# Eight-head cross-attention: where SP issues the weights of the next head among the spills and fetches

## The reference, cut to what matters

```python
Q = (img_embed @ Wq).reshape(B, -1, H, D).transpose(0, 2, 1, 3)
K = (sent_embed @ Wk).reshape(B, -1, H, D).transpose(0, 2, 1, 3)
V = (sent_embed @ Wv).reshape(B, -1, H, D).transpose(0, 2, 1, 3)
score = jnp.einsum('bhqd,bhkd->bhqk', Q, K) / math.sqrt(D)
score = jnp.where(mask, score, -jnp.inf)
attn = jax.nn.softmax(score, axis=-1)
ctx = jnp.einsum('bhqk,bhkd->bqhd', attn, V).reshape(B, -1, H * D)
out = ctx @ Wo + img_embed
# ... and a layer norm of out over the features
```

## Time and profile before

| | us |
|---|---|
| median of 3 runs | 522.12 |
| lowest, highest | 521.54, 522.39 |
| the profiled execution | 522.01 |
| its span | 520.2 |
| PE busy | 477.9 (92%) |
| DVE busy | 337.8 (65%) |
| ACT busy | 289.6 (56%) |
| POOL busy | 241.8 (46%) |

### The profile page before, as it was taken

One profiled execution on the slowest core, in us unless ns is written; L12 is line 12 of the kernel. 1 busy time (PEld: TensorE's weight loads), 2 busy tenths in 40 slices (PEclk: granted clock), 3 DMA queues, 4 the chain that ended last, 5 costly groups with the idle time before them and its releaser, 6 DMA issues.

```text
span 520.2 us, 7521 instructions
## 1 busy us (share of the span) xinstructions
PE 477.9 (92%) x2424; PEld 396.7 (76%) x2424; DVE 337.8 (65%) x681; ACT 289.6 (56%) x465; POOL 241.8 (46%) x136
## 2 busy tenths in 40 slices
PE   1989999987979999999999999999999999998992
PEld 0867787775868887888788878888888788777892
DVE  5999774655555657565756575667656675775357
ACT  4676475556554646565556565655656564635222
POOL 4646565438535353535353535363635453533004
PEclk9999999999989999999999999999999999999997
DMA  8313022678566566666566655665665665551002
GB/s 267 127 43 122 1 61 82 203 209 216 189 193 191 160 188 187 188 184 185 185 210 177 202 190 161 202 201 166 200 185 176 197 205 174 190 161 42 0 2 81
DMA packets 53975, 81.98 MB, mean 158 GB/s; under 512 B 5792, under 2 KB 43072, under 8 KB 53824
## 3 DMA queue, kind: packets, MB, share of 16 engines
q1 hardware_dynamic: 53632, 81.62, 51.2%
q10 hardware_dynamic: 320, 0.08, 0.1%
HBM read 49.16 MB, written 32.51 MB: 157 GB/s over the span
## 4 chain that ended last, share of the span: by engine, by line
PE 43%; issue 24%; POOL 15%; DVE 10%; ACT 4%; DMA 3%; SPq 1%; POOLq 0%; DVEq 0%; ACTq 0%
PE ps_scores L603 14%; POOL probs_t_lo L498 10%; POOL w_lo L430 3%; PE ps_o L625 3%; PE ps_o L629 3%; PE ps_o L627 3%; PE ps_o L628 3%; PE ps_o L626 3%; DMA ring<-in_weights_a 2%; PE ps_turn L619 1%; PE ps_task L551 1%; PE ps_task L553 1%; PE ps_task L552 1%; ACT probs L961 1%; DVE resid L1370 1%
## 5 line engine op out<-in xcount | busy, mean ns | idle before, releaser
L498 POOL TENSOR_TENSOR probs_t_lo<-probs_t_lo,probs_t_hi 128x1024 fp32r<-128x1024 f32 x60 | 143.8, 2397 | 197.5 <-ACT probs_t_hi L971 197.5
L971 ACT ACTIVATE probs_t_hi<-probs_t_lo 128x1024 fp32r<-128x1024 f32 x60 | 63.3, 1055 | 31.0 <-DMA probs_t_lo<-scratch 30.8
L625 PE MATMUL ps_o<-probs_t_hi,val_hi 128*128 128x512 f32 (+1 forms) x144 | 58.0, 403 | 8.0 <-POOL probs_t_lo L498 4.4
L1261 DVE RECIPROCAL row_inv<-row_sum 128x1 f32<-128x1 f32 x72 | 11.3, 159 | 75.4 <-PE ps_scores L603 67.2
L626 PE MATMUL ps_o<-probs_t_lo,val_hi 128*128 128x512 f32 (+1 forms) x144 | 56.8, 394 | 0.0
L629 PE MATMUL ps_o<-probs_t_lo,val_rem 128*128 128x512 f32 (+1 forms) x144 | 56.7, 394 | 0.0
L627 PE MATMUL ps_o<-probs_t_hi,val_lo 128*128 128x512 f32 (+1 forms) x144 | 56.7, 394 | 0.0
L628 PE MATMUL ps_o<-probs_t_hi,val_rem 128*128 128x512 f32 (+1 forms) x144 | 56.7, 394 | 0.0
L1298 DVE STREAM_TRANSPOSE probs<-probs 128x1024 f32<-128x1024 f32 x30 | 37.3, 1245 | 25.4 <-ACT probs L961 25.4
L603 PE MATMUL ps_scores<-key_hi,q_hi 128*128 128x512 f32 x144 | 46.6, 405 | 3.0 <-DVE neg_scores L1274 1.7
L1298 DVE STREAM_TRANSPOSE neg_scores<-neg_scores 128x1024 f32<-128x1024 f32 x30 | 37.2, 1241 | 13.9 <-ACT neg_scores L961 13.9
(11 more groups left out here) (247 smaller groups left out, 1096.7 us busy)
## 6 DMA issues: line engine op xcount, KB each, us to landing
probs_t_lo<-scratch SPq DMA_DIRECT2D x240, 128.0 KB, 2.9
scratch<-neg_scores SPq DMA_DIRECT2D x30, 512.0 KB, 3.8
scratch<-probs SPq DMA_DIRECT2D x30, 512.0 KB, 3.6
ring<-in_weights_a SPq DMA_DIRECT2D x9, 512.0 KB, 5.2
ring<-in_weights_b SPq DMA_DIRECT2D x9, 512.0 KB, 5.4
ring<-in_keys_t SPq DMA_DIRECT2D x4, 512.0 KB, 3.4
ctx_raw<-in_context SPq DMA_DIRECT2D x2, 768.0 KB, 9.5
ring<-in_context SPq DMA_DIRECT2D x16, 96.0 KB, 2.6
```

What stands on the lines that cost most here:

```text
L498: nc.gpsimd.tensor_tensor(pt_lo[b][:, t, :, :], pt_lo[b][:, t, :, :].bitcast(f32), pt_hi[b][:, t, :, :].bitcast(f32), ALU.subtract).then_i ...
L625: pe.matmul(o0, val_hi[b][:, kt, :], hi, start=first, stop=False)
L971: act.activation(pt_hi[b][:, t, :, :], pt_lo[b][:, t, :, :].bitcast(f32), ACT.Copy)\
```

## The change

In heads 1 to 6 the loads move to other places in SP's order. Before, A for the head after the next was issued behind `fetch(h, 4)` and B for the next head behind `fetch(h, 7)`. Now B for the running head is issued behind `fetch(h, 0)`, and A behind `fetch(h, 1)`. B for head 1, issued behind `fetch(0, 7)` before, goes behind `fetch(1, 0)`; B for the last head is issued behind `fetch(6, 5)`. In head 0 the places of `load_b(0)` and `load_a(1)` stay. The number of transfers, their bytes, the waits inside `load_a` and `load_b`, and all other engines' programs are unchanged.

```diff
                     fetch(h, j)
                     if h == 0 and j == 0:
                         load_b(0)
-                    if (j == 4 if h else j == 5) and h < HEADS - 2:
+                    if h and j == 0 and h < HEADS - 1:
+                        load_b(h)
+                    if (j == 1 if h else j == 5) and h < HEADS - 2:
                         load_a(h + 1)
-                    if j == 7:
+                    if h == HEADS - 2 and j == 5:
                         load_b(h + 1)
```

## The result

The changed kernel is slower: 538.84 us median of 6 runs (534.8 to 540.62) against 521.83 for the kernel before on the same chip (6 runs, 519.42 to 523.82), ratio 1.0327, 95% interval 1.0293 to 1.036. The forecast was 530.2 with a range of 523.5 to 535. The direction and the place were right, the size was not: +8.2 us were forecast and +17.0 came by the medians. The profiled execution took 540.41 us, 18.4 more than that of before.

A forecast was written before the change was run, and what follows sets the result against it. TensorE, busy 92%, was taken as the bound, so changes show as idle PE or lower clock. 522.01 - 7.0 (block 2) + 12.6 (waits at block 6) + 2.6 (clock) = 530.2 us, range 523.5 to 535.

The forecast's parts named there:

- the chain ahead of fetch 3: SP, heads 1 to 5: 22.3 us from gate to fetch 3; block 6 ready at gate + 30.45, wanted at 28.05.
- the clock behind the new gaps: PE after new waits at block 6: lower clock in head 1 and one of four others, 2 x 1.3 = 2.6 us.
- the plain pair of 5.5 us: SP's queue: fetch to fetch with a spill but no weights between takes 5.48 us, against 8.4 with weights.
- Part 1: Block 2, heads 1 to 6: block 7's weights leave, 8.9 us lost now, 1.9 kept in head 1, gain 7.0 us.
- the 1.9 forecast: Block 2 of head 1: PE still waits for the fetch issued at 140.40, 1.9 us lost with 0.2 for the gap.
- Part 2: Block 6, heads 1 to 5: both weights behind fetches 0 and 1 make waits, 3.0 + 4 x 2.4 = 12.6 us.
- The gate of 0.35 us: In an undisturbed head the fetch of block 0 goes out 0.35 us before scores of block 2.
- The last head: Block 2 of the last head: chain of 52.3 us against 52.7 for PE, so no wait.
- the gap of 1.51 us was followed by matmuls at the higher level: PE before 124.31 us: its matmul took 0.50 us, not the 0.77 behind the long gap of 3.05 us.
- The free place: Rival, chance 0.10: pairs with weights under 7.2 us, chain meets PE, only the 7.0 us gain is left, 515.0 us.
- The clock falls at every gap: Rival, chance 0.15: lower clock behind all five new gaps, 6.5 us in place of 2.6, total 534.1 us.

The follow-up runs named there:

- the second profile of the changed kernel: Changed kernel, unchanged, run again beside the kernel before on one chip: 533.57 us, ratio 1.032.
- the filler run: Changed kernel plus 8 extra unused matmuls on PE just before the value product of block 6 in heads 1 to 6: 530.35 us, ratio 1.026.
- half the bytes: Changed kernel with only columns 0 to 511 of 1024 of the weights of heads 1 to 6 loaded, at the same places: 515.08 us, ratio 0.9966.

## Why the prediction was right in kind and wrong in size

The direction and the mechanism, a wait at block 6 by the chain ahead of fetch 3, came true. Two terms of the sum failed: the clock behind the new gaps (2.6 us forecast, 7.8 measured), and the plain pair of 5.5 us, which took 7.2 to 7.5 in heads 1, 2 and 6.

**Part 1 (7.0 us forecast).** Block 2 of heads 2 to 6 lost 4.3 and now nothing; head 1 went from 4.55 to 0.7, its gap is 0.47 us. Together 8.2 gained. But this is a value of one profile: before, run again, loses 3.0 in all these places. The step behind it, a landing of 6.08 us in place of 4.5 with weights behind, is not a rule (the run with A behind fetch 3, and before, run again). And head 1's 0.7 in place of the 1.9 forecast is luck that was paid for in head 0: the clock fell there, PE came 1.6 us later to head 1 (its scores start at 133.79 and not at 132.16), and its wait shrank. In the second profile of the changed kernel, with no fall in head 0, block 2 of head 1 loses 1.7 us, near the forecast.

**Part 2, the mechanism.** Gate, pairs, landing, rounding, wait at block 6 of heads 1 to 5: all there. The gate of 0.35 us was measured at 0.35 to 0.36 in heads 2 to 6. Heads 3 to 5 had 22.0, 22.7 and 22.3 us to fetch 3 against 22.3, and lost 2.2, 3.0 and 2.5 us before the clock, against 2.4. Every experiment that took one set, or bytes, out of the chain ahead of fetch 3 took the waits at block 6 of heads 2 to 5 away; only in head 2 of two later runs did 0.2 and 1.7 us come back, behind a slow pair.

**Part 2, the size in heads 1 and 2 (a term of the sum).** The third pair, without weights, was forecast at 5.5 and took 7.47 in head 1 and 7.35 in head 2. So PE lost 5.2 in head 1 (3.7 at block 6, and 1.5 at blocks 4 and 5, nearly all of it by the minimum of block 5, which waits for spill 3) and 3.9 in head 2, against 3.0 and 2.4. The DMA view of the changed kernel from 165 to 172 us has spill 3 of head 1 in it (DMA share in tenths, GB/s, each in 40 slices, then the queues):

```profile
DMA  9999899689999989854000000000010000000001
GB/s 322 310 287 263 234 205 217 152 205 334 222 345 386 456 351 398 328 211 170 6 12 12 6 29 23 23 23 23 23 47 0 0 0 0 0 0 0 0 0 23
...
q8 instruction: 1, 0.02, 0.8%
...
scratch<-probs SPq DMA_DIRECT2D x1, 512.0 KB, 5.6
```

All but a trickle of 6 to 47 GB/s is over 3.3 us into the stretch, at 168.3; the trickle goes on for 2 us more, and the spill counts as landed only then, 5.6 us after issue, where the same spill in head 3 took 3.5. One transfer of instructions (q8) lies in that stretch. It lies in the 7.35 us pair of head 2 as well, and in the pair of fetches 6 and 7 of head 6 (7.25 us), and in no pair of 5.4 us of this trace. In the filler run, whose program for PE is longer, it falls in the pair before, and the third pair of head 2 takes 5.41. In other runs such a transfer also lay in pairs of 5.4, but there it came later. All 13 traces from head 1 on, for spills that SP issued right behind a fetch, with no weights between (us):

| from the issue of the spill to the start of q8 | from issue to landing | cases |
|---|---|---|
| 1.6 to 2.5 | 4.9 to 5.7 | 14 |
| 2.6 to 3.1 | 3.5 to 5.0 | 14 |
| 3.1 to 3.6 | 3.5 to 3.7 | 9 |
| none in the pair | up to 3.9 | the rest |

I take the late landing for one DMA engine that was held up by the instructions it moved. The order in time speaks for it, but no run moved or removed these transfers alone, so it is a likely cause and not a shown one.

**The last head (0 forecast, 1.9 measured).** The prediction had 52.3 us for the chain against 52.7 of PE. The pair of fetches 6 and 7 was in that sum with 5.5 us, took 7.25 as just said, and the pair with B ahead of it 9.00 and not 8.4; together that is over four times the half microsecond of room. With B one block earlier (518.71 us) the pair takes 5.51 us and the wait is gone, but so it is in the run with A behind fetch 3, where B stays. So the slow pair makes the wait, and the order isn't shown to make the slow pair.

**The clock (2.6 forecast, 7.8 measured).** This is the largest miss, 5.2 us. The step that failed is "the gap of 1.51 us was followed by matmuls at the higher level", from which I took four gaps of 2.2 to 2.4 us to be mostly safe. The changed kernel has that very gap in head 0, in a part that wasn't changed; timeline, then window:

```profile
124.45 0.79 PE L627 MATMUL ps_o<-probs_t_hi,val_hi 128*128 128x512 f32 x1 [1.50 <-POOL probs_t_lo L500]
...
124.00:128.00 4.00, 3.55 (x9) 2.83 (x10) 1.81 (x2) 2.71 (x6) 1.32 (x2) 0.57 0.58 183
```

The first matmul takes 0.79 us where it took 0.50 in the earlier trace rows, and the stretch has a clock of 0.57. The same gap left the clock alone in one execution and brought it down in another: over the 13 profiles, all with this gap of 1.5 us in head 0, the clock fell behind it in seven, and head 1 starts at 133.7 to 134.1 us in those that lost this time and at 132.2 to 132.6 in the six others. So 1.5 of the 18.4 us between the two profiles are chance and not the change, and 1.2 of them come back at block 2 of head 1 (part 1). In the changed kernel 2.00 us brought the clock down and 2.78 did not. One example of each kind is no bound; in the second profile even 3.29 us of idle left it alone, and of its five gaps at block 6 one brought the clock down. Each fall cost 1.5 to 1.7 us (1.7, 1.6, 1.5 and 1.6 in heads 1, 2, 3 and 5, 1.5 in head 0): the 1.3 forecast for one was near, the count was not.

**The rivals.** The free place would have come true at pairs under 7.2 us: half the bytes gave pairs of 6.7, no waits and a ratio of 0.9966, all of them 8.4 and 1.0327. (That the half weights took 515.08 us, the rival's 515.0, is luck, as before took 516.75 beside them.) "The clock falls at every gap" was nearer than the forecast in its count, four of five in the first profile, and still stopped at 534.1, for want of the slow pairs and of the fall in head 0.

**The sum.** -8.2 (forecast -7.0) + 16.8 for the waits of heads 1 to 5 (12.6) + 7.8 for the clock (2.6) + 1.9 (0) = 18.3 of 18.4 us. Of the difference of 10.1, the clock is 5.2, the waits 4.2, the last head 1.9, and part 1 gives 1.2 back.

## What to carry to other kernels

When a queue works as a chain that starts anew from a gate set by the critical engine, count what stands between the gate and the transfer that this engine needs next, and not the queue's load over the whole period: the same bytes cost nothing behind that transfer and, in heads 3 to 5 of the two profiles, 1 to 3 us a head in front of it. Large independent transfers that are spread so that each half of the period holds one cost least here, though no such order was clearly faster than the one before.

Price a gap of the matrix engine with its clock: after idle times of 1.5 us and more it fell here in some executions and not in others, and cost 1.5 us more each time. And don't call a chain safe that fits by half a microsecond: a spill landed 2 us late now and then, most likely behind a transfer of instructions.

## What the runs showed of the hardware that I had not expected

- The granted clock went to 1.2 GHz after 1.82, 1.92, 2.00, 2.33, 3.05, 3.35, 3.36, 3.48 and 3.68 us of idle PE ahead of a value product in heads 1 to 7 of the 13 profiles, and not after 1.93, 2.24, 2.78 and 3.29 nor after seven gaps of 1.59 to 1.78. Behind the gap of 1.5 us in head 0 it fell in seven of 13.
- With matmuls whose result is never used placed in the gap, the clock stayed up behind all five gaps, and the mean granted clock was 0.989 to 0.994 in four executions, against 0.977 to 0.987 in ten without them (the filler run).
- A transfer of 32 KB ahead of a spill on the same queue costs 0.1 us, 256 KB some 1.2 and 512 KB some 2.9.
- A spill of 512 KB landed after 5.6 us in place of 3.5, with a transfer of 16 KB of instructions in the same stretch and a trickle of 6 to 47 GB/s at the end. In 14 of 14 cases where such a transfer started 1.6 to 2.5 us behind the spill's issue, the spill took 4.9 us or more.
- A fetch with weights right behind it landed after 6.08 us in the first profile of the kernel before, after 4.35 in the run with A behind fetch 3, and after 4.97 at most in the kernel before, run again. The kernel before had medians of 516.8 to 517.0 us beside the experiments and 521.83 beside the changed kernel.
